# One core, a mixture-of-experts layer around attention: another calendar of transfers and blocks, routing cut into smaller pieces, and the zero experts' additions on GpSimd

## What is computed

```python
x = x + 0.5 * ffn(layernorm(x))
x = x + attention(layernorm(x))
x = x + 0.5 * ffn(layernorm(x))

def ffn(x):                                 # 8 experts with weights, 4 "zero" experts
    logits = x @ gate_w.T + expert_bias     # 12 columns
    topk_logits, topk_idx = top_k(logits, 2)
    w = softmax(topk_logits) at topk_idx
    h = silu(x @ w1[e].T);  y = h @ w2[e].T # for every chosen expert e < 8
    return sum_e w[e] * y[e] + (sum of w over the zero experts) * x
```

## Time and profile before

| | us |
|---|---|
| median of three runs | 1417.95 (1414.57 to 1418.41) |
| the profiled execution | 1431.64 |
| its span, first to last instruction | 1429.7 |
| PE busy in it | 1020.6 (71%) |
| DVE busy | 932.8 (65%) |
| ACT busy | 666.7 (47%) |
| POOL busy | 616.9 (43%) |
| mean granted TensorE clock | 0.868 |

### The profile page before, as it was taken

How to read it: one execution, slowest core, us unless ns; L and a number is a source line. 1 busy time by engine, 2 the same in 40 slices (tenths; PEclk the granted TensorE clock), 3 DMA queues, 4 the chain that set the end, 5 groups by cost and what they waited for, 6 DMA issues and landing times.

```text
span 1429.7 us, 37436 instructions
## 1 busy us (share of the span) xinstructions
PE 1020.6 (71%) x13558; PEld 664.5 (46%) x13558; DVE 932.8 (65%) x2505; ACT 666.7 (47%) x1356; POOL 616.9 (43%) x685
## 2 busy tenths in 40 slices
PE   1368176687768887878888888888888687764461
PEld 1347133374356444754445744444744474333340
DVE  6537466467556787678887878878788655634323
ACT  0246033365445545655556655555655554322441
POOL 2735146402634444454432444544335436544234
PEclk9978568789878899899999899999999988766676
DMA  8235811152154111631114521123611362131453
GB/s 249 65 99 118 256 50 52 50 114 76 47 116 113 51 48 53 137 100 52 53 43 94 132 59 57 46 65 81 130 58 52 101 141 66 46 81 41 104 125 86
DMA packets 248880, 125.29 MB, mean 88 GB/s; under 512 B 124384, under 2 KB 238925, under 8 KB 248448
## 3 DMA queue, kind: packets, MB, share of 16 engines
q1 hardware_dynamic: 232320, 94.01, 25.5%
q0 software_dynamic: 16384, 28.89, 8.2%
HBM read 36.25 MB, written 65.31 MB: 71 GB/s over the span
## 4 chain that ended last, share of the span: by engine, by line
PE 40%; DVE 22%; issue 14%; another core or an unknown queue 6%; ACT 5%; DMA 5%; SPq 4%; POOL 3%; DVEq 0%; POOLq 0%; ACTq 0%
PE banks L572 9%; DVE row_max L1278 9%; PE banks L601 5%; PE banks L547 3%; PE banks L445 3%; PE banks L447 2%; PE banks L539 2%; PE banks L446 2%; PE banks L404 2%; DMA x_cols<-xg 2%; PE banks L460 2%; PE banks L463 2%; PE banks L462 2%; ACT probs L806 2%
## 5 line engine op out<-in xcount | busy, mean ns | idle before, releaser
L806 ACT ACTIVATE probs<-banks 128x512 f32<-128x512 f32 x512 | 280.0, 595 | 338.0 <-PE banks L572 291.0
L887 POOL DMA_INDIRECT big<-yg,slots x256 | 253.9, 992 | 351.7 <-ACT y_rows L750 175.2
L873 POOL DMA_INDIRECT xg<-xs,slots x256 | 258.6, 1010 | 330.7 <-PE banks L572 238.0
L1278 DVE TENSOR_REDUCE row_max<-banks 128x2 f32<-128x512 f32 x512 | 330.6, 685 | 107.4 <-PE banks L572 76.5
L1167 DVE TENSOR_TENSOR h_lo<-h_f,h_hi 128x512 bf16<-128x512 f32 x198 | 135.9, 689 | 203.5 <-ACT h_hi L744 156.6
L601 PE MATMUL banks<-probs,v_op 128*32 128x256 f32 x2048 | 201.6, 408 | 12.3 <-issue 5.1
L460 PE MATMUL banks<-w_all,h_hi 128*128 x792 | 162.2, 232 | 57.5 <-DVE h_lo L1167 26.9
L547 PE MATMUL banks<-q_op,k_op 32*128 32x256 bf16 x1024 | 151.0, 288 | 61.2 <-issue 46.6
L742 ACT ACTIVATE h_f<-banks 128x512 f32<-128x512 f32 x198 | 118.8, 600 | 158.2 <-PE banks L447 102.9
L539 PE MATMUL banks<-k_op,q_in 32*128 32x256 bf16 x1024 | 154.4, 290 | 51.1 <-DVE row_max L1278 29.9
L572 PE MATMUL banks<-band_parts,thirds 96*32 96x296 bf16 (+2 forms) x4096 | 186.0, 289 | 1.7 <-issue 1.6
(11 more groups left out here) (170 smaller groups left out, 1635.9 us busy)
## 6 DMA issues: line engine op xcount, KB each, us to landing
yg<-y_rows SPq DMA_DIRECT2D x198, 128.0 KB
k_op<-kq_kept SPq DMA_DIRECT2D x96, 64.0 KB
q_in<-kq_kept SPq DMA_DIRECT2D x96, 64.0 KB
xg<-zeros SPq DMA_DIRECT2D x2, 2944.0 KB, 14.2
xg<-xs,slots POOLq DMA_INDIRECT x256
big<-yg,slots POOLq DMA_INDIRECT x256
kq_kept<-kq_hi SPq DMA_DIRECT2D x32, 128.0 KB
kq_kept<-kq_lo SPq DMA_DIRECT2D x32, 128.0 KB
```

The costliest lines, as they stand in the source:

```text
L806: act.activation(probs[:, q % 2, u % 4, :], banks[:, ST[(16 * b + u) % 3], :], ACT.Exp).then_inc(A["exp_done"], 1)
L873: pool.indirect_dma_start(xg[q], bass.IndirectOffsetOnAxis(slots[:, q % 4, c, t:t + 1], 0), xs[:, q % 2, t, :], None, bounds_check=groups[ ...
L887: pool.indirect_dma_start(y_back[:, i, c, :], None, yg[q], bass.IndirectOffsetOnAxis(slots[:, q % 4, c, t:t + 1], 0)).then_inc(gathered[i] ...
L1278: dve.tensor_reduce(row_max[:, gp, :, qt, j], banks[:, MX[v % 2], :].rearrange("p (k c) -> p k c", k=2), AX.X, ALU.max).then_inc(A["max_do ...
```

## The change

- **Calendar of blocks:** block 2 stands before turn 4 (it was 3), block 3 before 7 (5), block 4 before 11 (10). ADDS moves the combines accordingly.
- **Calendar of transfers:** POOL's indirect DMAs are spread by `spread(rows, q, t0, t1, b, steps, first)` over a given number of steps from turn b on. Gather 1 takes turns 0 and 1 (was turn 0), scatter 2 turns 2 and 3, the first four tiles of gather 2 half of turn 4, scatter 3 the next 20 steps, the rest of gather 2 stands beside block 3. Gather 6 stands wholly beside block 7 (32 transfers, were 24). Gather 7's first twelve tiles take 16 steps (were 12). Scatter 9 is paced over block 8's groups and the last four tiles of gather 7 over block 9's (`hi_ready`); gather 8's waits on the same counter stand behind those. Before, these three were unpaced.
- **Routing in pieces:** statistics, moments, roots and normalizing go in halves; in a block DVE does one half of a `token_norm` or one `token_parts` a step, PE turns tokens at every second group from 8 on and takes gate logits between, `first_choice` stands at group 16 of a 16-tile segment (was 13), slots at 21 (was 18).
- **Zero experts:** DVE computes z_scale = 1 + w_zero * rstd and z_bias = w_zero * rstd * mean per token (three small instructions a segment); POOL does x * z_scale - z_bias on each tile right behind its two scatters, 128 instructions in all. `add_zero_experts` is gone from DVE.
- **SP:** `store_out(7)` stands behind block 9's transfers; a block's first store waits only for the last user of the same buffer.

```diff
-    PHASES = {3: (2, 3), 5: (3, 4), 10: (4, 5), 17: (5, 6), 25: (6, 7), 29: (7, 8)}
-    ADDS = {-1: (0, 4, 8), 1: (1, 0, 8), 5: (2, 4, 8), 6: (2, 8, 12), 7: (2, 12, 16),
-            29: (6, 0, 4), 30: (6, 4, 12), 31: (6, 12, 16)}
-    for first, q in ((10, 3), (17, 4), (23, 5)):
+    PHASES = {4: (2, 3), 7: (3, 4), 11: (4, 5), 17: (5, 6), 25: (6, 7), 29: (7, 8)}
+    ADDS = {-1: (0, 4, 8), 0: (1, 0, 2), 1: (1, 2, 6), 2: (1, 6, 8), 4: (2, 0, 4), 7: (2, 8, 12), 8: (2, 12, 16),
+            29: (6, 0, 8), 30: (6, 8, 16)}
+    for first, q in ((11, 3), (17, 4), (23, 5)):
...
@@ sync @@
             experts(8)
+            experts(9)
             store_out(7)
-            experts(9)
...
@@ gpsimd @@
                             oob_is_err=False).then_inc(scattered[q % 2], 16)
+                    xt = tile_cols(SEG[q][0] + t)
+                    pool.tensor_scalar(xt, xt, z_scale[:, q % 2, t:t + 1], z_bias[:, q % 2, t:t + 1], ALU.mult,
+                                       ALU.subtract).then_inc(R["zero_added"], 1)
...
+            def spread(rows, q, t0, t1, b, steps, first=0):
+                n = 2 * (t1 - t0)
+                normed = b + (first > 5)
                 for t in range(t0, t1):
+                    at = [first + (2 * (t - t0) + c) * steps // n for c in range(2)]
+                    if normed * 8 + 6 <= b * 8 + at[0] and normed + 3 < NBATCH:
+                        batch_norm(normed + 3)
+                        normed += 1
...
+            def beside_block(rows, q, t0, t1, block, done="y_ready", root=True):
+                n = 2 * (t1 - t0)
+                ng = groups[block]
+                halves = list(range(SEG[block + 1][1] // 8)) if root else []
                 for i, t in enumerate(range(t0, t1)):
+                    after = [1 + (2 * i + c) * ng // n for c in range(2)]
+                    while halves and after[1] > 1 + 3 * halves[0]:
+                        token_root(block + 1, halves.pop(0))
+                    rows(q, t, t + 1, (C[done], G0[block] + after[0], G0[block] + after[1]))
...
-            two_a_step(gather_rows, 1, 0, 8, 0)
-            two_a_step(scatter_rows, 2, 0, 16, 1)
-            token_root(3)
-            two_a_step(scatter_rows, 3, 0, 16, 3)
-            beside_block(2, 0, 12, 3)
-            one_a_step(gather_rows, 2, 12, 16, 5)
-            one_a_step(scatter_rows, 4, 0, 16, 6)
+            spread(gather_rows, 1, 0, 8, 0, 16)
+            spread(scatter_rows, 2, 0, 16, 2, 16)
+            token_roots(3)
+            spread(gather_rows, 2, 0, 4, 4, 4)
+            spread(scatter_rows, 3, 0, 16, 4, 20, 4)
+            beside_block(gather_rows, 2, 4, 16, 3)
+            spread(scatter_rows, 4, 0, 16, 7, 32)
...
-            beside_block(6, 0, 12, 7)
-            two_a_step(scatter_rows, 8, 0, 8, 29)
-            two_a_step(gather_rows, 6, 12, 16, 30)
-            two_a_step(gather_rows, 7, 0, 12, 30, 4)
-            token_root(9)
-            scatter_rows(9, 0, 8)
-            gather_rows(7, 12, 16)
-            gather_rows(8, 0, 8)
+            beside_block(gather_rows, 6, 0, 16, 7)
+            spread(scatter_rows, 8, 0, 8, 29, 8)
+            spread(gather_rows, 7, 0, 12, 30, 16)
+            token_roots(9)
+            beside_block(scatter_rows, 9, 0, 8, 8, "hi_ready", False)
+            beside_block(gather_rows, 7, 12, 16, 9, "hi_ready", False)
+            beside_block(gather_rows, 8, 0, 8, 9, "hi_ready", False)
             gather_rows(9, 0, 8)
...
@@ vector @@
+                dve.tensor_scalar(z_scale[:, q % 2, 0:nt], z_gain[:, 0:nt], 1.0, None, ALU.add)
+                dve.tensor_tensor(z_bias[:, q % 2, 0:nt], z_gain[:, 0:nt], meanvar[:, 0:nt, 0], ALU.mult)
...
-            def add_zero_experts(q, k):
-                for t in range(4 * k, 4 * k + 4):
-                    xt = tile_cols(SEG[q][0] + t)
-                    i = dve.scalar_tensor_tensor(xt, xn[:, t, :], w_zero[:, t:t + 1], xt, ALU.mult, ALU.add)
-                i.then_inc(R["zero_added"], 1)
```

More of the change, by code:

```diff
@@ L317, in store_y @@
                 if g == 0 and q >= 2:
-                    sp.wait_ge(combined, T0[q - 1])
+                    used = max((i for i in range(q) if groups[i] == groups[q] and i % 2 == q % 2), default=-1)
+                    wait(sp, combined, T0[used + 1])
                 wait(sp, C["y_ready"], n + 1)
@@ L470, in experts @@
                 pe.wait_ge(R["owners_ready"], q + 1)
-                for g in range(max(ng + 2, 18 if nk else 0)):
+                f = 8 + 2 * nk if nk else 0
+                for g in range(max(ng + 2, f + 4 if nk else 0)):
                     if g == 0:
@@ L755, in experts @@
                 nk = SEG[nxt][1] // 4 if nxt else 0
-                for g in range(max(ng + 2, 17 if nk else 0)):
+                f = 8 + 2 * nk if nk else 0
+                for g in range(max(ng + 2, f + 4 if nk else 0)):
                     if g < ng:
@@ L947, in one_a_step @@
-            def one_a_step(rows, q, t0, t1, b):
-                for t in range(t0, t1):
-                    turn, at = b + (t - t0) // 4, 2 * ((t - t0) % 4)
-                    count = 16 * turn + 2 * at
-                    rows(q, t, t + 1, (A["st_done"], count + 2, count + 4))
-                    if at == 4 and turn + 3 < NBATCH:
-                        batch_norm(turn + 3)
-            def beside_block(q, t0, t1, block):
+                    at = [first + (2 * (t - t0) + c) * steps // n for c in range(2)]
@@ new lines, in spread @@
+                    if normed * 8 + 6 <= b * 8 + at[0] and normed + 3 < NBATCH:
+                        batch_norm(normed + 3)
+                        normed += 1
+                    same = at[0] == at[1]
+                    counts = [16 * b + 2 * at[0] + (1 if same else 2), 16 * b + 2 * at[1] + 2]
+                    rows(q, t, t + 1, (A["st_done"], *counts))
+                if normed * 8 + 6 <= b * 8 + first + steps and normed + 3 < NBATCH:
+                    batch_norm(normed + 3)
+            def beside_block(rows, q, t0, t1, block, done="y_ready", root=True):
+                n = 2 * (t1 - t0)
+                ng = groups[block]
+                halves = list(range(SEG[block + 1][1] // 8)) if root else []
@@ L1149, in route @@
                 token_slots(q)
-                for k in range(nk):
-                    add_zero_experts(q, k)
             def combine(q, t):
@@ L1385, in _ @@
             experts(9)
+            for t in range(12, 16):
+                combine(7, t)
             for t in range(SEG[8][1]):
```

133 lines of the change are left out of this document (67 added, 66 removed).

## The result

The changed kernel takes **1406.95 us** (median of 12 executions, 1400.93 to 1416.96), the kernel before beside it 1419.76 (12, 1414.57 to 1426.65): a ratio of 0.990 (95% interval 0.988 to 0.993). The direction was right; of the forecast 56 us 12.8 came, and the time lies 2 us above the range. Where single executions fell out of line (two of a3's nine, at 1497 and 1746 us, and one of the kernel before in each of the sets b and f), times and ratios are those of the others.

The account below looks back on a forecast made before the run. No engine is full; stages have different limits: bursts of routing, and dense indirect DMAs starving PE. Terms +4 - 3 - 18 + 3 - 12 - 5 - 25 = -56 took the median from 1417.95 to 1362 us, range 1325 to 1405.

Parts of the forecast that it names:

- The price of the addition: Zero experts' addition on POOL: 0.45 us a tile with dispatch, range 0.2 to 0.8.
- Start, +4: Start and block 0: sixteen additions between scatters 0 and 1 cost 4 us, range 0 to 8.
- Block 1, -3: Block 1: halved bursts and an earlier root save 3 us.
- Block 7, +3: Block 7: 32 gathers instead of 24 beside its groups cost 3 us net.
- Blocks 2 to 6, -18: Blocks 2 to 6: DVE is freed by 7.0 us a block, half counts; 18 us saved in all.
- Turns 0 to 10, -12: Turns 0 to 10 with gaps: transfers spread over more turns, 248.4 us against 260.6.
- Turns 11 to 28, 0: Turns 11 to 28: eight transfers and four additions a turn fit on POOL, no change.
- Turns 29 to 31, -5: Turns 29 to 31: turn 29 stays dense, 30 and 31 have 12 transfers instead of 16; 5 us saved.
- The end, -25: From block 8's first group to the end: paced transfers shorten blocks, tail grows to 47 us; about 25 us saved.
- Half of it: Rival, 1392 us, chance 0.20: block 8 stays at 42 us, turns with 13 transfers cost as much as with 16.
- Density is not the cause: Rival, 1413 us, chance 0.12: stalls of blocks 8, 9 and turn 3 stay, spacing brings nothing.
- The slower side: Rival, 1456 us, chance 0.07: a dear addition on POOL, 2.4 us, costs 94 more; decided from 1.6 us.

Follow-up runs that it names:

- a3: The kernel before with the routing in pieces alone (old calendar, additions on DVE): 1431.9 us, ratio 1.008.
- c4: The changed kernel with even tiles' additions by immediate scalars, odd tiles' as one multiplication by a per-partition scalar; results wrong; 1329.0 us in the one execution seen.
- a1: The changed kernel with the zero experts' additions back on DVE: 1409.2 us, ratio 0.992.
- c3: The changed kernel with eight y_rows tiles, gather 7's last tiles earlier, routing two groups earlier, weights and expert_bases in separate groups: 1284.3 us, ratio 0.995.
- d4: c3 with the zero experts' additions on DVE: 1257.2 us, ratio 0.973.
- b3: a1 with a memset on POOL that nothing reads behind each pair of scatters: 1409.3 us, ratio 0.992.
- d2: The changed kernel, unchanged, in a later set on a chip where both kernels run otherwise: 1344.5 us, ratio 1.041.
- b2: The kernel before with eight y_rows tiles instead of four and the routing in pieces: 1418.8 us, ratio 0.997.
- d1: The kernel before, unchanged, in a later set on the faster kind of chip: 1287.0 us in the one execution seen.
- b1: The kernel before with eight y_rows tiles instead of four: 1408.5 us, ratio 0.990.
- c1: b2 with the routing two groups earlier and weights and expert_bases in groups of their own: 1270.9 us, ratio 0.984.
- e1: c3 with the routing as late as in the changed kernel: 1297.0 us, ratio 1.006.
- a2: The changed kernel with the old calendar, routing in pieces and POOL's additions kept: 1414.6 us, ratio 0.998.
- d3: c1 run again in a later set: 1272.8 us, ratio 0.985.
- f1: d4 with the zero experts' additions of stages 4 to 9 on POOL: 1252.6 us, ratio 0.970.
- c2: c3 with the routing one group earlier instead of two: 1283.2 us, ratio 0.995.

## Why the prediction was wrong

The sum was to be 56 us and the profiled executions differ by 29; the other 16 us that the median lacks lie in which executions were profiled, as said with the result. I took the 13.7 us between the profiled execution and the median as something both kernels would have.

*The price of the addition* failed first: 0.81 us for 0.45. I took about the middle of two rows, a tensor_scalar of 128x2 with immediate scalars and an operation of 128x256 with two inputs; the one difference that counted, where the scalars come from (c4), is in none of them. The range's upper end, 0.8, was the truth. By itself it doesn't explain the time on this chip: with the additions back on DVE it is the same (a1). On the chip of c3 and d4 they cost 27 us.

*Start, +4*: -5.7. I counted the sixteen additions as work in POOL's chain and forgot my own reading of the end, that a dense run starves the block beside it: block 0 lies beside scatter 1, and there the additions are spacers (b3). On the chip of d2, without starvation, the bill is +7.9.

*Block 1, -3*: -1.5. *Block 7, +3*: +4.5. Right in direction and near in size.

*Blocks 2 to 6, -18*: +1.1. This is the largest failed step, "that frees 7.0 us ... I take half". DVE's work did fall by 4 us a block, but I never asked when the routing ends. The diff moves token_slots from group 18 to 21 of 23 and puts weights and expert_bases into one group, so the last h_lo come late, with nothing left for PE (order of time, b2), and the clock falls. And I did not price the ring of y_rows: ACT waited 17.1 us for it before, 45.2 after. Not all of the rise is the change's: where nothing starves, the kernel before waits 39.1 us for it (d1). With both undone blocks 2 to 6 take 238.9 us in c3 where d1 has 261.0, but that is not my forecast come true. Eight tiles alone take 14.0 us off them (b1), and moving the additions off DVE gives 15.2 (d4 to c3). That the pieces themselves ever save time no run shows: a3 has 1.4 us more in these blocks than before, b2 2.9 more than b1, and eight tiles in the old kernel were not run where before takes 1290 us, so c1's 249.9 can't be split. In the kernel before I took the waits of these blocks for the bursts' doing, and they were in part the ring's.

*Turns 0 to 10, -12*: -7.3. The turns came out shorter than forecast (0 to 2: 64.8 us), and the gap before block 2 is 19.3 us instead of 8.5, since sixteen pairs with an addition of 0.81 us don't fit into turns 2 and 3; POOL is what block 2 waits for. But these two cancel: from turn 2 to block 2 I forecast 63 us, it took 64.0, and without the additions 64.2 (a1). What the term lacked stands before blocks 3 and 4, gaps of 9.4 and 7.8 us for 6.5 and 5.5. *Turns 11 to 28, 0*: +8.5, which I had hidden under POOL's slack; but in d4, without these additions, they are only 2.1 us shorter than in c3, and the earlier routing gives more (4.1 from d2 to c3, 5.0 from e1 to c3): the larger part is again the late end of the routing. *Turns 29 to 31, -5*: -7.9.

*The end, -25*: -20.7. Block 8 was to take 28 and took 27.8, the gap 8.8 for 6.5, block 9 29.9 for 25 (whose own terms add to 23.1), the tail 43.4 for 47. The size was right for this chip, and that the spacing ends the stalls too. How it was reached was in part luck: I counted the additions in block 8 as no help, but with the same pacing and no additions it takes 35.4 us (a1), and with them and no pacing 26.9 (a2).

The rows, summed: -5.7 - 1.5 - 7.3 + 1.1 + 4.5 + 8.5 - 7.9 - 20.7 = -29.0 of 29.2.

*The rivals.* "Half of it" (1392) came nearest in time, but by another way than it told: block 8 was to stay at 42 us and took 27.8. "Density is not the cause" is refuted where I read the trace (b3, block 8 in a2) and holds on the chips of sets c to f: in d1 block 8 runs beside dense scatters undisturbed. There the trace agrees with the Trainium skill, "SBUF - State Buffer", Who interferes with whom, that DMA never contends with a compute engine. On the chips of a and b block 8 takes 55.3 and 55.2 us beside the same scatters (a3, b1); the page speaks of the ports of SBUF, and no run shows whether it is there that the engines are held up. The slower side came true there too (1.041), not by an addition of 1.6 us, but by one of 0.84 in the mean, where the spacing was worth nothing.

## What to carry to other kernels

Before a burst is cut into smaller pieces, ask at which group the last piece now ends and what the other engines still have to do there: a late end costs PE's idle time and then its clock. Price a GpSimd operation by a row with the same kind of scalars, and put it where no block waits for the transfers behind it. And when a gain comes from undoing a starvation whose cause the profile can't name ("issue", "another core or an unknown queue"), measure on a second chip, and at another hour, before keeping it.

## What the runs showed of the hardware

**Dense indirect DMAs starved the engines in some sets and not in others.** The same program took 1421 us in the earlier sets, on two chips and that of the result, and 1290 in the later ones, on three others. ACT's idle time that the trace puts down to something it can't see ("another core or an unknown queue"), in the kernel before where it takes 1421; d1 has no such row:
```profile
ACT probs L806 <- remote: 44.6, 26, 5.4
ACT h_f L742 <- remote: 25.3, 7, 8.4
ACT y_rows L750 <- remote: 24.8, 3, 14.5
```
All together it is 111 us on ACT and 49 on DVE against 0 and 0; PE's own unexplained idle is 105 us against 33, and the mean clock 0.869 against 0.90. In the changed kernel beside the result it is 35 and 17 us: most of it went, not all. What differs no run here tells, the chip or what else ran at the time; it stays open, as does why 0.8 us of other work between POOL's transfers relieves it.

**Per-partition scalars on GpSimd cost 0.3 us, and a second one with its operation 0.2 more,** for 128x128 float32: 0.32 us with immediates, 0.63 with one, 0.81 with two. With immediates it takes about what DVE's addition takes (0.34), with two such scalars 2.4 times as long.

**An idle of 2 us twice at a block's end was followed by a fall of PE's clock to 1.2 GHz** for some 12 us (b2, block 6); executions of b1 and b2, which differ in this among other things, had mean clocks of 0.871 and 0.854 and medians 10 us apart. Where the routing in pieces ends at group 21, the last 9 us of blocks 2 to 6 have a mean clock of 0.73 to 0.89 in every one of the eleven traces; where it ends at 19 (c1, c3, d3, d4, f1), 1.00. At group 20 (c2) it is 0.81 to 1.00, and the time is c3's.
